# Shifting the moving operands of a mixture of experts off the grid of its weights

## The reference

```
x = x + LN(mixer(LN(x)))          # mixer: project to 64 states, scan over time by a complex
                                  # rotation per state, project back, + D * u
x = x + LN(moe(LN(x)))
moe: g = x @ w_gate[e], u = x @ w_up[e]      # 8 experts, 128 -> 512
     h = silu(g) * u;  y[e] = h @ w_down[e]  # 512 -> 128
     out = sum over e of y[e] * cw[e]        # cw: normalised product of two softmaxes
```

## Time and profile before

| | before |
|---|---|
| median of 3 runs | 1175.03 us (1173.23 to 1175.30) |
| profiled execution, its own time | 1174.75 us |
| its span (first to last instruction) | 1172.9 us |
| busy: PE / PEld | 1143.5 / 943.3 us |
| busy: DVE / ACT / POOL | 928.8 / 677.4 / 636.2 us |
| mean granted clock of PE | 0.992 |

### The profile page before, as it was taken

How to read it: one execution, slowest core, us unless ns; L and a number is a source line. 1 busy time by engine, 2 the same in 40 slices (tenths; PEclk the granted TensorE clock), 3 DMA queues, 4 the chain that set the end, 5 groups by cost and what they waited for, 6 DMA issues and landing times.

```text
span 1172.9 us, 16867 instructions
## 1 busy us (share of the span) xinstructions
PE 1143.5 (97%) x5190; PEld 943.3 (80%) x5190; DVE 928.8 (79%) x2032; ACT 677.4 (58%) x1293; POOL 636.2 (54%) x496
## 2 busy tenths in 40 slices
PE   5899999999999999999999999999999999999996
PEld 4678888888888888888888888888888888888885
DVE  8788787787878878787887878778787887878665
ACT  3366565656556566565656656565655656556553
POOL 4467464555546455564655546455554645556453
PEclk8999999999999999999999999999999999999999
DMA  4230110101111020110101111010111102011110
GB/s 122 64 111 25 46 45 34 40 20 46 46 43 49 1 72 19 45 46 37 41 15 57 35 46 46 32 42 19 46 46 41 50 1 72 19 46 37 37 46 10
DMA packets 43097, 49.75 MB, mean 42 GB/s; under 512 B 3424, under 2 KB 24576, under 8 KB 43008
## 3 DMA queue, kind: packets, MB, share of 16 engines
q1 hardware_dynamic: 43008, 48.67, 13.4%
HBM read 44.20 MB, written 4.46 MB: 41 GB/s over the span
## 4 chain that ended last, share of the span: by engine, by line
PE 95%; DVE 3%; issue 1%; POOL 0%; ACT 0%; DMA 0%; POOLq 0%; SPq 0%; ACTq 0%; DVEq 0%
PE g L240 10%; PE u L240 10%; PE u L242 10%; PE u L241 10%; PE g L242 10%; PE g L241 10%; PE y L242 10%; PE y L240 10%; PE y L241 10%; PE n_ps L247 2%; PE m_ps L240 1%; PE m_ps L242 1%; PE m_ps L241 1%; PE y L263 1%; PE m_ps L321 1%
## 5 line engine op out<-in xcount | busy, mean ns | idle before, releaser
L982 POOL TENSOR_TENSOR hid_lo<-hid,hid_hi 128x512 fp32r<-128x512 f32 x255 | 342.2, 1342 | 394.5 <-ACT hid_hi L483 394.3
L477 ACT ACTIVATE gate<-g 128x512 f32<-128x512 f32 x512 | 306.3, 598 | 363.0 <-PE g L242 360.5
L723 DVE TENSOR_TENSOR hid<-gate,u 128x512 f32<-128x512 f32 x512 | 349.2, 682 | 176.9 <-ACT gate L477 121.6
L483 ACT ACTIVATE hid_hi<-hid 128x512 fp32r<-128x512 f32 x512 | 320.6, 626 | 29.4 <-DVE hid L723 28.7
L240 PE MATMUL g<-xe_hi,w_hi 128*128 128x512 f32 x512 | 207.8, 406 | 0.0
L729 DVE TENSOR_TENSOR hid_lo<-hid,hid_hi 128x512 fp32r<-128x512 f32 x257 | 205.7, 800 | 0.4
L240 PE MATMUL u<-xe_hi,w_hi 128*128 128x512 f32 x512 | 200.0, 391 | 2.3 <-DVE hid L723 2.3
L240 PE MATMUL y<-hid_hi,w_hi 128*128 128x512 f32 x512 | 199.8, 390 | 0.2 <-ACT hid_hi L483 0.2
L242 PE MATMUL y<-hid_hi,w_lo 128*128 128x512 f32 x512 | 199.8, 390 | 0.0
L242 PE MATMUL g<-xe_hi,w_lo 128*128 128x512 f32 x512 | 199.6, 390 | 0.0
L241 PE MATMUL g<-xe_lo,w_hi 128*128 128x512 f32 x512 | 199.6, 390 | 0.0
(11 more groups left out here) (155 smaller groups left out, 1146.6 us busy)
## 6 DMA issues: line engine op xcount, KB each, us to landing
cw_b<-cw_scratch SPq DMA_DIRECT2D x128, 256.0 KB, 3.6
x_sb<-x_in SPq DMA_DIRECT2D x16, 256.0 KB, 4.0
x_out<-o_sb SPq DMA_DIRECT2D x16, 256.0 KB, 2.3
stage<-wgate_in SPq DMA_DIRECT2D x8, 256.0 KB, 2.7
stage<-wup_in SPq DMA_DIRECT2D x8, 256.0 KB, 3.0
stage<-wdown_in SPq DMA_DIRECT2D x8, 256.0 KB, 3.6
cw_scratch<-cw_t SPq DMA_DIRECT2D x16, 16.0 KB, 1.4
proj<-proj_in SPq DMA_DIRECT2D x1, 136.0 KB, 2.5
```

What stands on the lines that cost most here:

```text
L477: nc.scalar.activation(gate[:, k % 2, :], g_ps[k % 2][:], ACT.Silu).then_inc(gate_ready, 1)
L483: nc.scalar.activation(hid_hi[:, k % RING, :], hid[:, k % RING, :], ACT.Copy).then_inc(hi_ready, 1)
L723: nc.vector.tensor_tensor(hid[:, k % RING, :], gate[:, k % 2, :], u_ps[k % 2][:], ALU.mult).then_inc(hid_ready, 1)
L982: nc.gpsimd.tensor_tensor(hid_lo[:, k % RING, :], hid[:, k % RING, :], hid_hi[:, k % RING, :].bitcast(f32), ALU.subtract).then_inc(lo_pool, 1)
```

## The change

Two things change. First, the moving buffers of the experts get a home that is 512 columns longer, and lie in it at an offset: `xe_hi` 64 columns (256 bytes), `xe_lo` 96 columns (384 bytes), `hid_hi` 2 columns (8 bytes), `hid_lo` 24 columns (96 bytes). The weights, and all other buffers, stay where they were relative to the 512-byte grid. No loop, order or wait of the units changes. Second, the prologue's dummies change: `keep_warm_mixed` goes, with the two DVE instructions and the semaphore that fed it, and `keep_warm(18)` stands in its place; 36 fp32r dummies of 496 moving columns, nine each with the weight 32, 64, 96 and 2 columns off, stand earlier, between `keep_warm(3)` and the first projection.

```diff
+XE_HI_AT, XE_LO_AT, HID_HI_AT, HID_LO_AT = 64, 96, 2, 24
+SHIFTS = (32, 64, 96, 2)
...
+        def shifted(name, n, at):
+            home = sb(name, [P, n * SEQ + SEQ], f32r)
+            return home[:, at:at + n * SEQ].rearrange("p (n t) -> p n t", n=n)
...
-        xe_hi, xe_lo = sb("xe_hi", [P, 2, SEQ], f32r), sb("xe_lo", [P, 2, SEQ], f32r)
+        xe_hi = shifted("xe_hi", 2, XE_HI_AT)
+        xe_lo = shifted("xe_lo", 2, XE_LO_AT)
...
-        hid_hi, hid_lo = sb("hid_hi", [P, RING, SEQ], f32r), sb("hid_lo", [P, RING, SEQ], f32r)
+        hid_hi = shifted("hid_hi", RING, HID_HI_AT)
+        hid_lo = shifted("hid_lo", RING, HID_LO_AT)
...
-            def keep_warm_mixed():
...
+            def keep_warm_shifted(shifts):
+                for o in shifts:
+                    for i in range(9):
+                        nc.tensor.matmul(y_ps[1][:, 0:SEQ - 16], proj_hi[:, o:o + P], act_hi[:, 0:SEQ - 16],
+                                         start=True, stop=True)
...
             keep_warm(WARM[1])
+            pe.wait_ge(act_hi_ready, 1)
+            keep_warm_shifted(SHIFTS)
             pe.wait_ge(proj_split, 2)
             mix_bu(0, prologue=True)
             keep_warm(WARM[2])
             mix_c(0)
             mix_turn_y(0, True)
-            keep_warm_mixed()
+            keep_warm(WARM[3])
             turn_tiles(1).then_inc(xe_turned, 1)
...
-            nc.vector.memset(hid[:, 0, :], 0.5).then_inc(flat_ready, 1)
-            dve.wait_ge(flat_ready, 1)
-            nc.vector.tensor_copy(hid_hi[:, 0, :], hid[:, 0, :]).then_inc(flat_ready, 1)
```

More of the change, by code:

```diff
@@ L146, in build @@
         w_hi_done, w_lo_done = sem("w_hi_done"), sem("w_lo_done")
-        const_ready, flat_ready = sem("const_ready"), sem("flat_ready")
+        const_ready = sem("const_ready")
         proj_split, omega_ready, trig_link, trig_ready = sem("proj_split"), sem("omega_ready"), sem("trig_link"), sem("trig_ready")
```

## The result

| | before | changed |
|---|---|---|
| median, both measured side by side | 1175.16 us | 1190.67 us (1189.33 to 1190.94) |
| ratio | 1 | 1.0132, 95% interval 1.0114 to 1.0149 |
| span of the profiled execution | 1172.9 us | 1189.2 us |
| busy: PE / DVE / ACT / POOL | 1143.5 / 928.8 / 677.4 / 636.2 us | 1168.9 / 920.7 / 674.5 / 576.7 us |
| mean granted clock of PE | 0.992 | 0.995 |

The changed kernel is 1.3% slower. 3.9 ns x 4608 is 18.0 us.

A forecast was written before the change was run, and what follows sets the result against it. The prediction took PE and its matmul pitch as the bound. From the profiled 1174.75 us, -0.1 for the prologue and 4608 x 0 for the shifts gave 1174.65; the median lies 0.3 above, so it predicted 1174.7 us, range 1155 to 1191.

The forecast's parts named there:

- The bound, PE and its pitch: Whole run: PE is the bound, and 4608 expert matmuls times the change in their 0.2267 us pitch decides.
- I take zero for all four shifts, by the rows nearest to it (16 and 32 bytes): Expert matmuls: the four address shifts change the pitch by nothing, 4608 x 0, judged from prologue dummies at 0.225 us.
- Not of the relative place of the two operands: Expert matmuls: the surplus of 0.011 us over 0.216 belongs to the moving stream, not the operands' relative place.
- The short weight load: Prologue dummies loading 32 weight columns, not 128: at 0.225 us no cheaper, taken as evidence against load and stream colliding.
- The rival of the broken rhythm: Units: the buffers' different shifts break PE's even pitch in each unit, up to +20.8 us, 1195.5; chance 0.09.
- The rival of pieces of 64 bytes: y matmuls: `hid_hi` and `hid_lo` starts cost one more 64-byte piece, `xe` nothing; +10.2 us, 1185; chance 0.22.
- The rival of collisions taken away: Expert matmuls: the surplus is colliding reads that the shifts remove, up to -50.7 us, 1124; chance 0.23 in all.
- The prologue: Before the units: new dummies fill PE's 9.12 us idle stretch and keep its clock up; -0.1 us.
- They delay nothing: Prologue: the 36 dummies end by 20.8 to 21.4 us, before `act_lo` is ready at 22.01, 0.6 us to spare.
- The cover of the other engines: Units: a lag of three units, about 5.5 us, hides slower writes of `hid_hi` and `hid_lo`; cost nothing.
- TensorE's two ports in SBUF are independent: Expert matmuls: the skill's rule that loading weights takes nothing from the running matmul's reads; counted against any gain.
- The 16-byte line: Matmuls reading `hid_hi`: 8 bytes off means 129 lines for 128, at most 1.7 ns on 1024 matmuls, +1.7 us.

The follow-up runs named there:

- xe alone: Changed kernel with `hid_hi` and `hid_lo` back at offset 0, `xe_hi` at 256 and `xe_lo` at 384 bytes: 1181.86 us, ratio 1.0065.
- the trains: Kernels without the computation: 108 matmuls of the kernel's pattern per arrangement, from resting buffers; 226.67 ns each at no offset, 231.1 with the changed offsets.
- turns_off: Changed kernel, its offsets of 256, 384, 8 and 96 bytes kept, moving columns read in turns of 4 (0 4 1 5 2 6 3 7): 1133.32 us, ratio 0.9649.
- hid alone: Changed kernel with `xe_hi` and `xe_lo` back at offset 0, `hid_hi` at 8 and `hid_lo` at 96 bytes: 1191.84 us, ratio 1.0145.
- turns_line: As turns_off, but `hid_hi` at 16 bytes in place of 8 (offsets 256, 384, 16 and 96): 1125.01 us, ratio 0.9575.

## Why the prediction was wrong

- **The bound, PE and its pitch:** right. Nothing but the pitch decided, and the arithmetic of 4.6 us a nanosecond held.
- **"I take zero for all four shifts, by the rows nearest to it (16 and 32 bytes)":** this is the step that failed. The zero came from eight dummies at 225 ns. They had 504 columns, one pairing only, and there were four of each. 108 matmuls of 512 columns settle at 231.6 with 16 bytes and 233.3 with 32, and a common shift of 16 bytes costs the kernel 18 us. What looked like "no effect of the shift" was read from matmuls of another size; the changed kernel's own dummies, of 496 columns, show hardly any effect of 8 and 384 bytes either. The term put at zero is 4608 x 3.9 ns = 18.0 us.
- **"Not of the relative place of the two operands":** wrong. Both moved by 64, 96 or 128 bytes is free, one alone isn't. The short weight load, which I read at 225 from two pitches, settles at 231.7; it did not bear what I drew from it. That the surplus hangs on the moving stream too was right: one repeated column (216.1) and the order of reads (215.8) take it away.
- **The rival of the broken rhythm, +20.8 us at most, 1195.5, chance 0.09:** nearest in time, and its place (g and u lengthened as well as y) was seen. Its mechanism holds only in part: the shifted kernel settles in a pattern of its own, and a common shift of 16 bytes costs as much without any mixing. That 1190.67 lies just under the upper end of 1191, which was set by half of this rival, is luck.
- **The rival of pieces of 64 bytes, +10.2, 1185:** fell. Its sign was right; its rule (y alone, xe free) was not, since xe alone costs 6.9 us, and a common shift of 64 bytes costs 2.2 ns a matmul.
- **The rival of collisions taken away, down to 1124:** no shift gave anything. The prize was real: it came with the order of reads, at 1124.74. That its size came out so well is in part luck, for it was read off float32 dummies of 256 recorded columns, which read `ident` twice; only the trains show 215.83 for an fp32r matmul of 512 columns.
- **The prologue:** right within what can be told. Forecast -0.1 us; with shifts that cost nothing the whole measured 0.9992 (0.9983 to 1.0002). The first g starts at 44.91 us before and at 43.93 in the changed profile, but with the same prologue at 43.77 (xe alone) to 45.45 us (turns_off), so this 1.0 us shows nothing. "They delay nothing" failed in the changed profile by the 1.5 us told above, off the path.
- **The cover of the other engines:** right; PE's waits for them in the units did not grow. (The lag is three units of 2.04 us, 6.1 us and not 5.5; the margin was larger than I had it.)
- **"TensorE's two ports in SBUF are independent"** (the Trainium skill, "TensorE: Matmul & The Clock Gate", its step-by-step of a matmul), which I weighed against a gain: the runs disagree with it as a rule on time. Shifting the weight alone by 128 bytes takes the pitch from 226.67 to 233.4 ns, the moving operand alone to 232.3, and both together leave it at 226.67. The same page of the Trainium skill has N / 2.4 + 2.5 ns, 215.8 at 512 columns; it agrees with the reads in turns, 215.83, and not with any plain read of 512 different columns. The prediction called the float32 dummies' 216 an agreement, but they have 256 columns in the record, for which the formula gives an estimate of 109 ns.
- **The 16-byte line** (the Trainium skill, "SBUF — State Buffer", in the section on the DMA port swizzle), which I priced at +1.7 us: the unit is seen in the runs, where order within 16 bytes is free and a run of four across two lines costs 12 ns in the reads in turns. But one line more, 129 for 128, was an estimate of 1.7 ns at most; all four buffers at 8 bytes cost 6.7 and at 4 bytes 10.0. And that each step to a new line costs, as the Trainium skill has it there, the runs bear out for strides of 2 to 64 columns (431 to 487 ns) and contradict for turns between two lines, a new line at every column and the fastest read of 512 different columns.

What stays open is the inner cause: why a plain stream pays 11 ns, and up to 22 with a shift, which a stream in turns between two lines does not, and which rule in bytes gives the price of a shift (252 bytes is free, 240 costs most of those above 128). A collision with the weight load is a guess: the load's place matters, but a weight load of 32 columns or of one repeated column raised the pitch and did not lower it. No run separates a matmul from its load.

## What to carry to other kernels

When matmuls in fp32r bind, look at the pitch first: at 512 columns, more than 216 ns on the trace is a surplus that addresses or the order of reads may decide, 11 ns of 227 here. Keep the moving operand and the weight a multiple of 256 bytes apart and both on a grid of 64 bytes (both off by 16 cost 6.7 ns), or better, read the moving columns in turn from two 16-byte lines, with each run of four inside one line, and hide the reordering in what is written rarely, not in the ring that every unit writes. Do not take a bound from a few matmuls of another size: a train of a hundred costs 25 us in a kernel of its own.

## What was not expected of the hardware

- The pitch settles into patterns that repeat. In many plain trains the sum over nine is a whole multiple of 6.67 ns: 9 x 226.67 = 306 x 6.67 on the grid, 9 x 231.11 = 312 x 6.67 as changed; in others (236.67, 215.83) it is not. In the kernel before, PE is back in its pattern ten matmuls after a transposition.
- POOL's subtraction into `hid_lo` takes 1137 ns with `hid_hi` at 8 bytes in the changed kernel, 1140 with hid alone shifted and 1157 in turns_off, and 1338 to 1356 with it at 0, 16 or 256, `hid_lo` at 96 bytes in one of these (turns_line). So it is the 8 bytes; why it is faster there is open. PE did not wait for it in the changed kernel.
- A stride of 1 KB in ACT's write to SBUF nearly doubles it (626 to 1137 ns), while TensorE's reads in the same turns are even faster than plain ones.
